# Causal convolution attention with a mixture of experts: the experts' down weights split on VectorE and behind the gathered rows, the last expert's products reordered

## The reference, cut to what matters

```python
xg = xpad[buf]                                   # [16 experts, 256 slots, 512]
gact = jax.nn.silu(jnp.einsum('ech,ehi->eci', xg, w_gate))      # i = 352
mid = gact * jnp.einsum('ech,ehi->eci', xg, w_up)
eout = jnp.einsum('eci,eih->ech', mid, w_down) * wbuf[..., None]
y = jnp.zeros((T + 1, h), x.dtype).at[buf.reshape(-1)].add(eout.reshape(-1, h))[:T]
shared = jax.nn.silu(x @ sw_gate) * (x @ sw_up) @ sw_down
return (y + shared).reshape(b, s, h)
```

## Time and profile before

| What | Value |
|---|---|
| median of three runs | 693.52 us |
| time of the profiled execution | 693.3 us |
| its span, first to last instruction | 691.5 us |
| mean granted TensorE clock | 0.967 |
| PE busy | 616.1 us (89%) |
| DVE busy | 567.5 us (82%) |
| ACT busy | 282.0 us (41%) |
| POOL busy | 434.7 us (63%) |
| first gate and up products of expert 0 | at 430.41 us |

### The profile page before, as it was taken

One profiled execution on the slowest core, in us unless ns is written; L12 is line 12 of the kernel. 1 busy time (PEld: TensorE's weight loads), 2 busy tenths in 40 slices (PEclk: granted clock), 3 DMA queues, 4 the chain that ended last, 5 costly groups with the idle time before them and its releaser, 6 DMA issues.

```text
span 691.5 us, 14342 instructions
## 1 busy us (share of the span) xinstructions
PE 616.1 (89%) x4487; PEld 571.8 (83%) x4487; DVE 567.5 (82%) x1248; ACT 282.0 (41%) x503; POOL 434.7 (63%) x499
## 2 busy tenths in 40 slices
PE   2856998999999999999998888998999999999990
PEld 2846896998989989999898676988988888888880
DVE  5899989769889889788899687988888888888740
ACT  3422542423433424234241144355465565544640
POOL 4875697566766667576721116477667777777662
PEclk9987999999999999999999899999999999999996
DMA  6572512404225224131210326766767777776434
GB/s 168 175 212 85 183 32 78 136 33 129 86 61 152 61 78 134 61 91 56 71 57 1 91 96 205 252 180 194 208 193 200 202 216 227 218 207 186 104 39 54
DMA packets 50373, 90.12 MB, mean 130 GB/s; under 512 B 3921, under 2 KB 20305, under 8 KB 50337
## 3 DMA queue, kind: packets, MB, share of 16 engines
q1 hardware_dynamic: 43168, 72.89, 34.0%
q0 software_dynamic: 7168, 16.78, 11.6%
HBM read 72.71 MB, written 16.94 MB: 130 GB/s over the span
## 4 chain that ended last, share of the span: by engine, by line
PE 51%; issue 20%; DVE 15%; ACT 6%; POOL 4%; DVEq 2%; DMA 1%; SPq 0%; ACTq 0%; POOLq 0%
PE gu L527 15%; PE yb L464 14%; PE gu L552 8%; PE gu L656 5%; PE mb L444 3%; ACT ew L865 3%; PE mb L671 2%; DVE ew L1473 2%; DVE prod L1187 2%; PE yb L656 2%; DVE mid L1489 1%; DVE xgT L1481 1%; DVE prod L1190 1%; DVE oT L1206 1%; POOL midl L1009 1%
## 5 line engine op out<-in xcount | busy, mean ns | idle before, releaser
L464 PE MATMUL yb<-kvh,toep 128*128 128x288 f32 x640 | 141.4, 308 | 10.5 <-DVE prod L1190 10.5
L527 PE MATMUL gu<-xT,sw 128*128 128x256 f32 (+2 forms) x1152 | 143.2, 283 | 3.7 <-issue 3.1
L527 PEld LDWEIGHTS gu<-xT,sw 128*128 128x128 f32 (+2 forms) x1152 | 138.8, 182 | 4.5 <-issue 4.1
L1206 DVE TENSOR_REDUCE oT<-prod 128x256 f32<-128x2048 f32 x32 | 123.8, 3870 | 0.1
L464 PEld LDWEIGHTS yb<-kvh,toep 128*128 128x128 f32 x640 | 110.6, 199 | 12.3 <-issue 10.7
L1001 POOL TENSOR_TENSOR kvl<-kv,kvh 128x1152 fp32r<-128x1152 f32 x31 | 83.4, 2689 | 52.0 <-ACT kvh L753 51.9
L1473 DVE TENSOR_TENSOR ew<-raw_w,ew 128x704 fp32r<-128x704 f32 x64 | 108.5, 1700 | 4.6 <-ACT ew L865 4.6
L993 POOL TENSOR_TENSOR kv<-kT 128x256 f32 (+3 forms) x248 | 111.2, 490 | 0.0
L464 PE MATMUL yb<-kvl,toep 128*128 128x288 f32 x320 | 97.9, 306 | 0.0
L1187 DVE TENSOR_TENSOR prod<-yb,qT 128x96 f32<-128x96 f32 (+11 forms) x288 | 78.1, 282 | 22.8 <-PE yb L464 21.2
L1009 POOL TENSOR_TENSOR midl<-mid,midh 128x256 fp32r<-128x256 f32 x40 | 33.3, 835 | 74.6 <-ACT midh L769 64.5
(11 more groups left out here) (170 smaller groups left out, 1084.8 us busy)
## 6 DMA issues: line engine op xcount, KB each, us to landing
toep<-toeplitz_taps SPq DMA_DIRECT2D x32, 512.0 KB, 3.7
raw_w<-in_L_ffn_w_gate_dram SPq DMA_DIRECT2D x16, 704.0 KB
raw_w<-in_L_ffn_w_up_dram SPq DMA_DIRECT2D x16, 704.0 KB
raw_d<-in_L_ffn_w_down_dram SPq DMA_DIRECT2D x16, 512.0 KB
c_t<-in_ctx_dram SPq DMA_DIRECT2D x16, 256.0 KB, 4.6
x_t<-in_x_dram SPq DMA_DIRECT2D x16, 256.0 KB, 5.1
normalised_tokens<-xn SPq DMA_DIRECT2D x16, 256.0 KB, 3.0
out_dram<-yo SPq DMA_DIRECT2D x16, 256.0 KB, 2.9
```

Source lines behind the costliest of these rows:

```text
L464: last = pe.matmul(yb[:, lb, 0:PW], toep[s][:, a, d:d + P], rhs[:, s, m, :], start=(i == 0), stop=(i == len(steps) - 1))
L527: last = pe.matmul(gu[0:m, i % 2, u * GT:(u + 1) * GT], sw[:, c, a, col:col + m], xT[:, c, b, :], start=(c == 0 and (a, b) == PASSES[0]), ...
L1206: dve.tensor_reduce(oT[:, :, hl * HD * B:(hl + 1) * HD * B], prod[:, s, :, :, :].rearrange("p c i w -> p c w i"), AX.X, ALU.add)\
```

## The change

The low parts of the down weights (`low_d`) go from GpSimd's list to the end of VectorE's unit. ACT rounds the down weights (`split_d`) behind `round_rows` instead of at the front of the unit. In VectorE's unit `low_w` 0 to 2 come earlier (also in unit 0, for `low_w` 2), `decode` comes ahead of the second `e_middle`, and `low_rows` and the fourth `low_w` ahead of the second `e_low`. The last unit becomes a function of its own on three engines, in which TensorE puts the down products of expert 14 behind the first block of expert 15.

```diff
@@ tensor engine: @@
+            def last_unit(e, k):
+                expert_gu(e, k, 0)
+                expert_down(e - 1, 1 - k)
+                expert_gu(e, k, 1)
+                expert_gu(e, k, 2)
+                expert_down(e, k)
...
-            unit(E - 1, 1, True, False, False)
-            expert_down(E - 1, 1)
+            unit(E - 2, 0, True, False)
+            last_unit(E - 1, 1)
@@ scalar engine: @@
-                split_d(e, k)
-                if next1 and not (isinstance(e, int) and e == 0):
+                if not (isinstance(e, int) and e == 0):
                     for c in range(LB):
                         split_w(e + 1, 1 - k, c)
                 e_silu(e, k, 0)
                 e_round(e, k, 0)
                 e_silu(e, k, 1)
                 e_round(e, k, 1)
...
+                round_rows(e + 1, 1 - k)
+                split_d(e, k)
                 if before:
                     weigh(e - 1, 1 - k)
...
+                e_silu(e, k, 2)
+
+            def last_unit(e, k):
+                e_round(e - 1, 1 - k, 2)
+                split_d(e, k)
+                e_silu(e, k, 0)
+                e_round(e, k, 0)
+                weigh(e - 1, 1 - k)
+                for j in range(1, EJ):
+                    e_silu(e, k, j)
+                    e_round(e, k, j)
+                weigh(e, k)
@@ gpsimd: @@
-            def low_d(e, k):
-                pool.wait_ge(ed_h, e + 1)
-                wait(pool, e_dn, HALVES * e - HALVES)
-                pool.tensor_tensor(ed[k][:, 0:2, 1, :], raw_d[k][:, 0:2, :], ed[k][:, 0:2, 0, :].bitcast(fp32),
-                                   ALU.subtract)
-                pool.tensor_tensor(ed[k][0:EK[2], 2, 1, :], raw_d[k][0:EK[2], 2, :],
-                                   ed[k][0:EK[2], 2, 0, :].bitcast(fp32), ALU.subtract).then_inc(ed_l, 1)
-
             def unit(e, k, before, next2):
-                low_d(e, k)
@@ vector engine: @@
+            def low_d(e, k):
+                dve.wait_ge(ed_h, e + 1)
+                wait(dve, e_dn, HALVES * e - HALVES)
+                dve.tensor_tensor(ed[k][:, 0:2, 1, :], raw_d[k][:, 0:2, :], ed[k][:, 0:2, 0, :].bitcast(fp32),
+                                   ALU.subtract)
+                dve.tensor_tensor(ed[k][0:EK[2], 2, 1, :], raw_d[k][0:EK[2], 2, :],
+                                   ed[k][0:EK[2], 2, 0, :].bitcast(fp32), ALU.subtract).then_inc(ed_l, 1)
+
+            def unit(e, k, before, next2):
+                late = not (isinstance(e, int) and e == 0)
...
                 if late:
                     low_w(e + 1, 1 - k, 0)
+                    low_w(e + 1, 1 - k, 1)
                 e_middle(e, k, 0)
-                if late:
-                    low_w(e + 1, 1 - k, 1)
+                low_w(e + 1, 1 - k, 2)
                 e_low(e, k, 0)
                 keep_slots(e, k)
-                e_middle(e, k, 1)
                 if next2:
                     decode(e + 2, k)
+                e_middle(e, k, 1)
+                low_rows(e + 1, 1 - k)
+                low_w(e + 1, 1 - k, 3)
                 e_low(e, k, 1)
-                if next1:
-                    low_w(e + 1, 1 - k, 2)
-                    low_rows(e + 1, 1 - k)
-                    low_w(e + 1, 1 - k, 3)
...
+                low_d(e, k)
                 if isinstance(e, int) and e == 0:
                     values(4, E)
+
+            def last_unit(e, k):
+                e_middle(e - 1, 1 - k, 2)
+                e_low(e - 1, 1 - k, 2)
+                low_d(e, k)
+                keep_slots(e, k)
+                for j in range(EJ):
+                    e_middle(e, k, j)
+                    e_low(e, k, j)
```

More of the change, by code:

```diff
@@ L674, in expert_down @@
                     last.then_inc(e_dn, 1)
-            def unit(e, k, before, next1, next2):
+            def unit(e, k, before, next2):
                 expert_gu(e, k, 0)
@@ L680, in unit @@
                     slots(e + 2)
-                if next1:
-                    rows_t(e + 1, 1 - k)
-                else:
-                    expert_gu(e, k, 2)
+                rows_t(e + 1, 1 - k)
                 if before:
                     expert_down(e - 1, 1 - k)
-                if next1:
-                    expert_gu(e, k, 2)
+                expert_gu(e, k, 2)
[3 more added lines that the diff above has]
+                expert_gu(e, k, 1)
+                expert_gu(e, k, 2)
+                expert_down(e, k)
             slots(0)
@@ L694, in _ @@
             rows_t(0, 0)
-            unit(0, 0, False, True, True)
-            unit(1, 1, True, True, True)
+            unit(0, 0, False, True)
+            unit(1, 1, True, True)
             with pe.Fori(1, E // 2 - 1) as i:
-                unit(2 * i, 0, True, True, True)
-                unit(2 * i + 1, 1, True, True, True)
-            unit(E - 2, 0, True, True, False)
-            unit(E - 1, 1, True, False, False)
-            expert_down(E - 1, 1)
+                unit(2 * i, 0, True, True)
+                unit(2 * i + 1, 1, True, True)
+            unit(E - 2, 0, True, False)
+            last_unit(E - 1, 1)
         @block.scalar
@@ L900, in e_round, with unit @@
                 act.activation(midh[0:m, EJ * k + j, :], mid[0:m, s, :], ACT.Copy).then_inc(e_midh, 1)
-            def unit(e, k, before, next1):
+            def unit(e, k, before):
                 if before:
                     e_round(e - 1, 1 - k, 2)
-                split_d(e, k)
-                if next1 and not (isinstance(e, int) and e == 0):
+                if not (isinstance(e, int) and e == 0):
                     for c in range(LB):
@@ L912, in unit @@
                 e_round(e, k, 1)
[L913 to L917, removed]
+                round_rows(e + 1, 1 - k)
+                split_d(e, k)
                 if before:
                     weigh(e - 1, 1 - k)
-                if next1:
-                    e_silu(e, k, 2)
+                e_silu(e, k, 2)
[9 more added lines that the diff above has]
+                weigh(e, k)
             for i in range(SJ):
@@ L935, in _ @@
             act.wait_ge(dn_mm, TT * NG)
-            unit(0, 0, False, True)
-            unit(1, 1, True, True)
+            unit(0, 0, False)
+            unit(1, 1, True)
             with act.Fori(1, E // 2 - 1) as i:
[L939 to L943, removed]
+                unit(2 * i, 0, True)
+                unit(2 * i + 1, 1, True)
+            unit(E - 2, 0, True)
+            last_unit(E - 1, 1)
         @block.gpsimd
@@ L1497, in e_low, with unit @@
                                    midh[0:m, EJ * k + j, :].bitcast(fp32), ALU.subtract).then_inc(e_midl, 1)
-            def unit(e, k, before, next1, next2):
-                late = next1 and not (isinstance(e, int) and e == 0)
+            def low_d(e, k):
[5 more added lines that the diff above has]
+                                   ed[k][0:EK[2], 2, 0, :].bitcast(fp32), ALU.subtract).then_inc(ed_l, 1)
+            def unit(e, k, before, next2):
+                late = not (isinstance(e, int) and e == 0)
                 if before:
```

4 lines of the change are left out of this document (removed).

## The result

The changed kernel is slower: 733.87 us in the median of four runs (732.42 to 736.04) beside 693.59 (691.5 to 695.0) for the kernel before on the same chip, a ratio of 1.0595 [1.0567, 1.0622]. The prediction said 678.0 (675 to 686). The profiled execution took 734.9 us, its span is 732.9, the mean granted clock 0.935.

A forecast was written before the change was run, and what follows sets the result against it. VectorE's stall in `low_w` beside GpSimd held units at 15.44 us; without it TensorE bounds at 14.22. Second to fifteenth units fall from 215.8 to 200.0, so 693.3 - 15.8 = 677.5, plus 0.5 for the clock: 678.0 us, range 675 to 686.

The forecast's parts named there:

- The stall: VectorE's `low_w` takes 4.78 us beside GpSimd's down-weight low parts, median 0.892; all 64 were to be near 0.9.
- The 1.8 of the sum: Cost per unit of the two down-weight low-part subtractions on VectorE, in us; bounds 0.89 and 4.8.
- the 75 forecast: GpSimd's busy time was to go down by about 75 us.
- u1: Second expert's unit, where TensorE waits 1.4 us for `one_hot`: 15.7 us, before 15.4.
- u14: Second to last expert's unit, which has no `slots`: 13.7 us.
- the tail: Last unit: 1.35 us gained, taken back by a wait with slower clock; taken as 0, bounds -1.35 and +0.2.
- its 0.5 for the clock: Added to the time for half of a possible clock drop, 0 to 1.5 us, after the second unit's wait.
- rival B: At `keep_slots`, the wait for the scatter's landing takes the stall's place: 687 us; chance 0.15.
- 2.8 us of slack: Time by which the next unit's inputs on VectorE, ending with the fourth `low_w`, were to be ahead of TensorE's 14.2.
- C: Raw weights behind the down weights in SP's queue come late: for example 8 us slower, 702; chance 0.04.
- D: VectorE's stall is not GpSimd's doing or comes back, `low_w` staying long: within 693 +- 3; chance 0.06.
- E: Shorter new TensorE waits drop the clock in several units, 3 or 4 times 1.5 us: 683; chance 0.09.

The follow-up runs named there:

- e7_four_buffers: Changed kernel with four buffers instead of two for the copied indices and weights, `keep_slots` waiting for a scatter two experts further back, loops over four units: 676.42 us, ratio 0.9744.
- e5: Changed kernel in which experts 2 to 15 load only a piece of their raw weights, the rest left out: 714.42 us, one run.
- e9: Changed kernel with a drain on VectorE behind the single `one_hot`: 735.73 us, ratio 1.0613.
- e12: Changed kernel with both a drain behind `one_hot` and most raw loads of experts 2 to 15 left out: 698.29 us, one run.
- e13: Changed kernel with all loads kept, SP loading the raw gate and up weights ahead of the raw down weights: 712.38 us, ratio 1.0276.
- e2: Changed kernel with `split_d` put back at the front of ACT's unit: 707.38 us, ratio 1.023.
- e4: Kernel before with only `low_d` moved, from GpSimd to the end of VectorE's unit: 734.52 us, ratio 1.061.
- e10: Kernel before with four buffers of the copied indices and weights and nothing else: 691.62 us, ratio 0.9985.
- e1: Changed kernel with `keep_slots` and `decode` behind `low_d`, and on GpSimd the scatter ahead of the gather: 786.65 us, ratio 1.1352.
- e3b: Changed kernel with `one_hot` done twice, a VectorE drain between the two: 720.18 us, one run.

## Why the prediction was wrong

**The stall** (point by point, first what held). `low_w` is at 0.89; the two new subtractions take 1.22 and 0.68 (forecast 1.2 and 0.65), 1.90 together. The 1.8 of the sum doesn't follow from its own terms: with a fixed part of 0.07 they give 1.93; nothing hangs on it. GpSimd freed its pair, 75.2 us, but its busy time fell by 35.5 (434.7 to 399.2) and not by the 75 forecast, since its scatter issues took 101.0 in all and not 52.9. u1 took 15.57 (15.7), u14 13.7 (13.7), the tail 22.2 (21.95 with no gain). In e7_four_buffers TensorE's unit is 14.13 (14.22) and the time 676.4 (678.0). So the whole sum was right for a kernel in which `keep_slots` doesn't wait, to 1.6 us (its 0.5 for the clock is called half of 0 to 1.5, which would be 0.75), and so was the taking of 0 for the last unit: there TensorE did wait 1.87 us, and the clock fell, 0.73 in the mean of 655 to 660.

**The step that failed** is the wait at `keep_slots`. The sum puts it at nothing, with units of 14.22, on the ground that rival B gives: "`keep_slots` at 7.1", "7.0 at the median", "2.8 us of slack", and a price of 687 at worst. The wait measured 82.4 us, 6.1 a unit in the loop, and the units 19.1. Rival B had the right place, wait and sign of the mechanism, and the wrong form. Three things in it:

1. *The slack.* It set the landing against TensorE's unit, as if `weigh` stood fixed at 12.7. But `weigh` stands behind the second product, the row rounding and `split_d` on ACT, and these behind `keep_slots`: each late landing delays the next scatter by as much. Such a ring has no slack of 2.8; its length against 14.22 decides. Its part from `keep_slots` to the first issue is 6.33, so already at the best prices, 6.33 + 1.93 + 5.6 = 13.9, the slack was 0.3. And with B's own prices (issue held until 3.35, landing after 7.3, so 11.15 after an issue near -0.5) the ring is 6.33 + 11.15 = 17.5. That is 3.3 over TensorE's unit, 12 times, so 717 us: slower, where the prediction's B was a milder gain. The 6.33 is measured in the changed kernel; the prediction's own places give nearly the same, 13.7 - 7.1 = 6.6, so this sum could have been made before the run.
2. *The issue.* B left the first issue free and held the second until `one_hot` ends; by that, the first would take 2.8 here (574.03 to 576.82). It took 5.42 to 5.58 in all of u2 to u13. In the earlier trace rows one sees 2.51, since there the issue came in the middle of `one_hot` and only a short instruction followed before VectorE paused. e5 shows that loads don't do this, e9 and e12 that a pause in VectorE's row shortens it; in u14, without `one_hot`, the issue took 1.75.
3. *The queues.* "Against: the loads were there before too" was wrong in time: with `low_d` on VectorE, SP's loads are released just as the scatter goes out (the last one 2.4 us behind the first issue, before 2.2 ahead of it), and the landing grows from 5.8 to 7.3. e13, whose only edit sends two thirds of the loads out earlier, shows it.

**`split_d` behind the row rounding** was put at nothing, since `weigh` waited for the down products anyway. In the ring it stands ahead of `weigh` and costs: without it there (e2) the unit is 2.3 shorter, with the better place of the issue in it. It isn't what made the kernel slower, though: e4 has it at the front too, and 734.5 us.

**The rule of the Trainium skill in the prediction** ("SBUF — State Buffer", section "Who interferes with whom") is that the two engines contend for shared ports, which are an exclusive lock. That page of the Trainium skill states the lock for the whole instruction beside VectorE's two-port modes, and the prediction took it over to instructions with two SBUF inputs. By it the issue, which came first, would keep the ports for its 1.6 us, and `one_hot` would wait. The trace agrees that the two engines hold each other up, and not in the form: `one_hot` began at 574.54 and took its usual 2.28, and it was the issue that took 5.43, beyond the end of `one_hot` at 576.82 and of the four instructions behind it.

**Rivals C, D and E.** No wait for raw weights showed (C), `low_w` isn't long (D). The half clock came (E), behind waits of 2.00 to 4.53 us in nine units, and not behind waits of 1.72, 2.35 and 2.63, but off the chain.

**Before the change** the ring was some 0.4 us under the unit in the unit shown, and e10 shows that it wasn't the bound. The change removed what hid it, and lengthened it in the same step.

## What to carry to other kernels

Where an instruction waits for a transfer so as to reuse a buffer, follow what it releases until you come back to it: if you do, and it is closed once a unit, the unit can't be shorter than that loop, however much each engine idles. Its length is read from rows of the loop, not from waits, for a stalled instruction ahead of the wait hides it. Before work is moved, give such a wait more buffers: here four in place of two turned a change of +6% into one of -2.5% (675.6 to 676.6 us in three kernels, below both originals), for four more small tiles and a loop body of four units. Three buffers weren't tried.

## What the runs showed of the hardware

- A GpSimd issue of a scatter took 1.55 us alone and 5.43 us where a VectorE row without a pause began with `one_hot` 0.51 us behind its start; second issues took up to 7.30 in e1 and e7. With a pause of 0.1 to 0.2 us put behind `one_hot` it took 4.29, in each of the units 2 to 12 of e9 and e12, and ended 1.5 us after `one_hot`: as if the issue's whole work began there. That reading is argued, not shown, and e4 speaks against a pause right there as the condition: its issue of 4.42 also ended 1.5 us after `one_hot`, with the next instruction following at once and the pause only behind that one.
- Nor does overlap alone do it. With `one_hot` 0.50 us behind the start an issue took 4.29 or 1.75 in units of one kernel (e3b), and in e1 a second issue took 1.57 with `one_hot` 0.28 behind its start and 7.24 with 0.11. Why the 5.43 ended where no gap is seen, and which boundary between instructions counts, stays open.
- The time from the second scatter issue to its landing was 5.1 to 5.5 us with few raw loads, 5.1 to 5.6 with 2 MB of them of which the last gate and up load went out 6.9 ahead (e13), and up to 9.7 with the same loads in other places. Between kernels it was the longer, the later these loads were issued beside the scatter (the table's last column); within one kernel it still varied by up to 2.7 (e9).
- A gain in one part of a ring can be eaten by another: in e9 1.1 us less in the issue, no change in the time.
